# First layer's attention: ScalarE writes the fp16 high halves of two of five weight blocks by a second exponential

## The reference, cut to what matters

```python
q = (hidden_states @ Wq).reshape(b, s, NUM_HEADS, HEAD_DIM)       # 4, 512, 32, 16
kv = hidden_states @ Wkv
k, v = (kv[..., :HEAD_DIM], kv[..., HEAD_DIM:])
scores = jnp.einsum('bqhd,bkd->bhqk', q, k) * scale
bias = slopes[:, None, None] * (pos[None, None, :] - pos[None, :, None])
scores = jnp.where(causal[None, None], scores + bias[None], -jnp.inf)
attn = jax.nn.softmax(scores, axis=-1)
out = jnp.einsum('bhqk,bkd->bqhd', attn, v).reshape(b, s, h)
return out @ Wo
...
x = x + _layernorm(_L0_attn_ref(_layernorm(x, axis=-1), L0_attn_Wq, L0_attn_Wkv, L0_attn_Wo), axis=-1)
x = x + _layernorm(_L0_ffn_ref(_layernorm(x, axis=-1), ...), axis=-1)
```

## Time and profile before

| | us |
|---|---|
| median of three runs | 2361.22 |
| all three | 2360.77, 2361.22, 2366.06 |
| the profiled execution | 2361.95 |
| its span, first to last instruction | 2360.2 |
| busy TensorE / VectorE / ScalarE / GpSimd | 2064.3 / 1772.9 / 1393.0 / 961.4 |

### The profile page before, as it was taken

The page is one execution under the profiler, slowest core; times in us unless marked ns, Lnnn a source line. Parts: engine busy times, 40 slices in busy tenths (PEclk is TensorE's granted clock), DMA queues, the critical chain, the costliest instruction groups (busy, mean ns, idle before and its releaser), DMA issues. The chain is left out here.

```text
span 2360.2 us, 46322 instructions
## 1 busy us (share of the span) xinstructions
PE 2064.3 (87%) x17280; PEld 1236.9 (52%) x17280; DVE 1772.9 (75%) x3704; ACT 1393.0 (59%) x3030; POOL 961.4 (41%) x966
## 2 busy tenths in 40 slices
PE   7576687878765579999999999999999999988998
PEld 3244455555542245666656665656665666543444
DVE  5577888888765367787778787877787878877665
ACT  3344455564544367777778777777777777752222
POOL 1056766776783133323332333332333333343221
PEclk9788898989887799999999999999999999999999
DMA  6101010100101333543545344434444444430000
GB/s 228 39 10 32 15 45 15 46 13 13 40 1 45 108 73 69 95 86 68 95 86 95 74 80 93 88 68 91 84 96 70 87 82 85 86 94 19 36 18 36
DMA packets 394816, 153.70 MB, mean 65 GB/s; under 512 B 363152, under 2 KB 374032, under 8 KB 392544
## 3 DMA queue, kind: packets, MB, share of 16 engines
q1 hardware_dynamic: 394592, 150.73, 29.5%
HBM read 48.69 MB, written 11.53 MB: 26 GB/s over the span
## 5 line engine op out<-in xcount | busy, mean ns | idle before, releaser
L1629 POOL TENSOR_TENSOR q_in_sbuf<-q_in_sbuf,sinq 128x512 f32<-128x512 f32 x128 | 162.6, 1271 | 724.6 <-ACT q_in_sbuf L1761 603.0
L1773 ACT ACTIVATE xp<-xp,nm 128x128 f32<-128x128 f32 (+3 forms) x512 | 281.3, 550 | 200.4 <-DVE nm L1854 200.4
L789 ACT ACTIVATE weights<-bank,unit 128x512 f32<-128x512 f32 x320 | 210.5, 687 | 269.7 <-PE bank L592 268.3
L1738 ACT ACTIVATE probs_hi<-xp,rl 128x128 f16<-128x128 f32 (+3 forms) x512 | 245.1, 550 | 64.8 <-DVE rl L1874 64.8
L1825 DVE SCALAR_TENSOR_TENSOR probs_lo<-xp,rl,probs_hi 128x128 f16<-128x128 f32 (+3 forms) x512 | 282.5, 613 | 0.0
L513 POOL CAST weights_hi<-weights 128x1024 f16<-128x1024 f32 (+1 forms) x192 | 213.0, 1122 | 157.0 <-ACT weights L789 139.6
L1833 DVE TENSOR_TENSOR q1T_lo<-qf,q1T_hi 128x512 f16<-128x512 f32 x128 | 88.4, 691 | 227.8 <-ACT q1T_hi L1752 227.8
L1854 DVE CUSTOM_DVE_ANT_0 xp<-bank,mask,cs 128x128 f32<-128x128 f32 (+3 forms) x512 | 250.4, 545 | 0.0
L1655 PE MATMUL bank<-p1T_hi,v_hi 128*128 128x128 f16 x1280 | 221.5, 219 | 2.6 <-DMA p1T_lo<-probs_lo 2.6
L1655 PE MATMUL bank<-p1T_hi,v_lo 128*128 128x128 f16 x1280 | 221.4, 219 | 0.0
L1655 PE MATMUL bank<-p1T_lo,v_hi 128*128 128x128 f16 x1280 | 221.4, 219 | 0.0
(11 more groups left out here) (317 smaller groups left out, 5795.2 us busy)
## 6 DMA issues: line engine op xcount, KB each, us to landing
raw_q<-in_wq SPq DMA_DIRECT2D x8, 1024.0 KB, 6.3
raw_o<-in_wo SPq DMA_DIRECT2D x8, 1024.0 KB, 6.4
x_front<-in_x SPq DMA_DIRECT2D x4, 1024.0 KB, 5.7
q_stack<-q_hi SPq DMA_DIRECT2D x256, 16.0 KB, 1.8
xb<-in_x SPq DMA_DIRECT2D x4, 1024.0 KB, 5.2
wup<-in_wup SPq DMA_DIRECT2D x3, 1024.0 KB, 11.2
fused_scratch<-fused SPq DMA_DIRECT2D x12, 256.0 KB, 2.9
x_scratch<-xb SPq DMA_DIRECT2D x3, 1024.0 KB, 4.3
```

Source lines behind the costliest of these rows:

```text
L789: act.activation(px[:, p % 2, i, :], bank_of(("x", p, i))[:, :], ACT.Exp, scale=unit[:, 0:1]).then_inc(s_ed, 1)
L1629: pool.tensor_tensor(qs[:, i % 2, :], qs[:, i % 2, :], rope["sink" if u[0] == "k" else "sinq"][:, :], ALU.mult).then_inc(s_rot, 1)
L1738: ins = act.activation(pr[0][:, m % 2, c], xp[:, m % 3, c], ACT.Copy, scale=rl[:, m % 3, t:t + 1])
L1773: ins = act.activation(x, x, ACT.Exp, scale=-1.0, bias=nm[:, m % 3, t:t + 1], accum_out=ls[:, m % 3, t:t + 1])
```

## The change

ScalarE writes blocks 3 and 4 of a pair twice: once as fp32 into `px`, and once more, by the same exponential of the same bank, as fp16 into `ph[0]`. GpSimd then casts only blocks 0 to 1 and 2, and subtracts for blocks 3 and 4 in one call of 1024 columns. VectorE's second subtraction is only block 2, 512 columns. The waits follow: ScalarE waits at block 3 for GpSimd's low halves of the pair two before, and for that pair's value products, since it now writes `ph[0]`; GpSimd waits for the fifth exponential instead of its own casts; a pair has two casts to count, not three.

```diff
                 def weights_hi(p):
                     if p >= 2:
                         pool.wait_ge(s_pf, p - 1)
-                    for i, (c0, c1) in enumerate(((0, 2), (2, 4), (4, 5))):
+                    for c0, c1 in ((0, 2), (2, 3)):
                         pool.wait_ge(*emptied[("x", p, c1 - 1)])
                         pool.tensor_copy(ph[0][:, p % 2, c0:c1, :], px[:, p % 2, c0:c1, :]).then_inc(s_wh, 1)
-                    pool.wait_ge(s_wh, 3 * p + 3)
-                    pool.tensor_tensor(ph[1][:, p % 2, 4, :], px[:, p % 2, 4, :], ph[0][:, p % 2, 4, :],
+                    pool.wait_ge(*emptied[("x", p, 4)])
+                    pool.tensor_tensor(ph[1][:, p % 2, 3:5, :], px[:, p % 2, 3:5, :], ph[0][:, p % 2, 3:5, :],
                                        ALU.subtract).then_inc(s_wc, 1)
...
                 def exponential(p, i):
-                    if p >= 2 and i in (0, 2, 4):
-                        act.wait_ge(*((s_wl, 2 * (p - 2) + 1), (s_wl, 2 * (p - 2) + 2), (s_wc, p - 1))[i // 2])
+                    if p >= 2 and i in (0, 2, 3):
+                        act.wait_ge(*{0: (s_wl, 2 * (p - 2) + 1), 2: (s_wl, 2 * (p - 2) + 2), 3: (s_wc, p - 1)}[i])
+                    if p >= 2 and i == 3:
+                        act.wait_ge(s_pf, p - 1)
                     act.wait_ge(*filled[("x", p, i)])
-                    act.activation(px[:, p % 2, i, :], bank_of(("x", p, i))[:, :], ACT.Exp,
-                                   scale=unit[:, 0:1]).then_inc(s_ed, 1)
+                    ins = act.activation(px[:, p % 2, i, :], bank_of(("x", p, i))[:, :], ACT.Exp, scale=unit[:, 0:1])
+                    if i >= 3:
+                        ins = act.activation(ph[0][:, p % 2, i, :], bank_of(("x", p, i))[:, :], ACT.Exp,
+                                             scale=unit[:, 0:1])
+                    ins.then_inc(s_ed, 1)
...
                 def weights_lo(p, i):
-                    c = slice(2 * i, 2 * i + 2)
-                    dve.wait_ge(s_wh, 3 * p + i + 1)
+                    c = slice(2 * i, 2 + i)
+                    dve.wait_ge(s_wh, 2 * p + i + 1)
```

## The result

The changed kernel takes 2369.39 us (median of 11 runs, 2367.82 to 2372.73) against 2362.22 us before (11 runs, 2356.94 to 2366.06). The ratio is 1.0035, with a 95% interval of 1.0026 to 1.0043: slower by 7.2 us. The profiled execution has a span of 2366.1 us, 5.9 more than before.

A forecast was written before the change was run, and what follows sets the result against it. VectorE, 83% busy, was taken as nearest to the bound, with ScalarE's copy order and SyncE's DMA queue as other chains. The terms -11.6 + 14.3 + 5 gave +7.7 us, hence 2369 us; range 2346 to 2386.

The forecast's parts named there:

- VectorE's gain, -11.6: First layer's attention after 276 us: VectorE's shorter second subtraction releases TensorE earlier in some steps, 11.6 us saved.
- the rival's 20: Rival A's gain: 0.57 us counts in 83% of the 42 steps after 276 us, 20 us in all.
- ScalarE's order, +14.3: Extra exponentials stand before ScalarE copies that VectorE and TensorE wait for, in the first layer's attention: 14.3 us lost.
- The port, +5: VectorE's subtractions and GpSimd's longer 2.2 us subtraction exclude each other: 5 us lost, bounds -10 and +25.
- rival C: The port lock dominates: VectorE's first subtraction meets GpSimd's 2.2 us block, mean above 1.6 us; 2389 us; chance 0.08.
- 36 or more: Sign expected in the profile after: VectorE's busy time down 36 us or more.
- two signs of being wrong: First: VectorE's waits for ScalarE's high halves not growing about 0.5 us each; second: SyncE's chain binding after 276 us too.
- upper bound of +25: Port term's upper bound: half a microsecond lost in each of 50 steps, 25 us.
- A: VectorE is the bound and ScalarE's slack real: 2341 us, or 2349 in a half form; chance 0.22 with that form.
- B: Losses on ScalarE and port equal the gains within 7 us: 2361, between 2354 and 2368; chance 0.30.

The follow-up runs named there:

- third run: The kernel before with only VectorE's second subtraction cut to block 2, ScalarE and GpSimd unchanged: 2347.78 us, ratio 0.9949.
- the split one: GpSimd's 1024-column subtraction made in two calls of 512: the changed kernel so edited took 2366.98 us, and without ScalarE's second exponentials 2351.99 us.
- the fills: The changed kernel without second exponentials, GpSimd's subtraction replaced by two fills of the same 1024 columns that read nothing: 2346.52 us, ratio 0.9928.
- first run: The kernel before with ScalarE's second exponentials of blocks 3 and 4 added alone, written to an unread tile: 2382.99 us, ratio 1.0097.
- fourth: The changed kernel with ScalarE's second exponentials moved behind the copies that follow the first ones, same instructions: 2360.82 us, ratio 1.0002.
- second run: The changed kernel without ScalarE's second exponentials, GpSimd's 1024-column subtraction kept: 2360.97 us, ratio 1.0001.
- eighth: The changed kernel with second exponentials behind the copies and GpSimd's subtraction in two calls of 512: 2351.23 us, ratio 0.9956.
- sixth: The changed kernel without second exponentials and with GpSimd's subtraction in two calls of 512: 2351.99 us, ratio 0.9959.

## Why the prediction was right, and which terms were not

**The total.** Forecast 2369, measured 2369.39. The directions were right, but two terms were off by 6 to 8 us each, in opposite directions. That the total fits to half a microsecond is luck.

**VectorE's gain, -11.6.** Right. Alone it is -12.8 us, though the third run's higher clock (0.9492 over all its runs, 0.946 before) has a part in that. The 512-column call takes 0.67 to 0.68 us where nothing blocks it, where I took 0.65, and the gain is far below the rival's 20, as TensorE waits for VectorE only in some steps.

**ScalarE's order, +14.3.** The mechanism is right: the waits for the high halves grew by 16.2 us, 11.9 of them by the second exponentials, the order alone takes 8.6 us of the loss away, and the waits go with it. The size depends on what stands beside it. Adding the second exponentials costs 2369.39 - 2360.97 = 8.4 us beside GpSimd's one long call, and 2366.98 - 2351.99 = 15.0 beside the split one. That the 14.3 is close to the second figure doesn't help it, since the changed kernel has the one long call.

**The port, +5.** This is the step that was mis-sized: "I count 0.3 to 0.8 us in a third of 50 steps, 5 us". Without the second exponentials it is 13.2 us, and 14.4 by the fills, the lower clock included. I looked only at the two big subtractions, and between them the waits did not grow: in the changed kernel's trace the group lost 185.2 - 144.7 = 40.5 us, more than 64 x 0.57 = 36.5. The mean of the first stayed at 1482 ns, below the 1600 that I had named as rival C's mark. Without the second exponentials, where the 13 us were measured, the 512-column form does wait, with a mean of 944 ns. And in both I missed tiny VectorE instructions that read one small tile, before and after:

```profile
L968 DVE COPY mx<-mp 128x8 f32<-128x8 f32 x15 | 8.9, 596 | 0.6 <-DVE mx L966 0.2
L890 DVE TENSOR_SCALAR ve<-mv 128x4 f32<-128x4 f32 x14 | 4.1, 292 | 0.5
```

```profile
L973 DVE COPY mx<-mp 128x8 f32<-128x8 f32 x15 | 13.9, 926 | 0.6 <-DVE mx L971 0.2
L895 DVE TENSOR_SCALAR ve<-mv 128x4 f32<-128x4 f32 x13 | 10.5, 807 | 0.4
```

Together 13.0 us became 24.4. The first of them feeds the maxima's transpose, the second the norms, so both stand at the head of a chain. Without the second exponentials they are 13.0 and 9.5 us, with fills in place of the subtraction 6.8 and 5.1. How much of the 13 us they make, beside the 16.5 us of the big subtractions and the clock, is not shown. My sum had no term for the clock at all.

**How they fit.** Why is the sum -13 + 13 + 8 and not -13 + 13 + 15? A likely reason: the second exponential delays the long call by 0.58 us, and in the last steps VectorE's 512 columns are then over before it begins. In the changed kernel these rows stand so, VectorE and then GpSimd:

```profile
696.94 0.67 DVE L965 TENSOR_TENSOR weights_lo<-weights,weights_hi 128x512 f16<-128x512 f32 x1
...
697.22 2.38 POOL L515 TENSOR_TENSOR weights_lo<-weights,weights_hi 128x1024 f16<-128x1024 f32 x1 [3.08 <-ACT weights_hi L793]
```

GpSimd is the one that waits here. VectorE's 512-column calls sum to 49.9 us in the changed kernel and to 60.4 without the second exponentials, 10.5 more, which fits. That this is the whole of the 7 us is argued, not shown. So the total came out right because a port term too small by 8 us met a ScalarE term too large by 6.

**The signs.** The second exponentials are there, 128 with a mean of 689 ns, and VectorE's 512-column call takes 0.68 us unblocked. VectorE's busy time, though, fell by 27.3 us and not 36 or more (469.96 to 442.70, from 120 us to the last copy of head sums), since the tiny instructions took 11.4 of the 40.5 us back and others some more. Of the two signs of being wrong, the first did not come: the waits for high halves grew by 0.46 us each. The second did in part. After 276 us TensorE waited 6.9 us in 4 places for the maxima's DMA before, at most 2.6, and waits 14.2 in 6 now, the longest here:

```profile
607.01 0.61 PE L590 MATMUL bank<-q_stack,k_stack 128*128 128x512 f16 x1 [5.51 <-DMA q_stack<-m_lo]
```

The third run, with VectorE's part alone, has such a wait of 5.46 us too. So SyncE's queue can bind after 276 us as well once VectorE is faster, and my gain had no term for that. The range was also narrower than the prediction says: with the port at its upper bound of +25 its own sum gives 2389, outside 2386.

**The rivals.** A is refuted by the first run: alone ScalarE's work costs 22 us. Its slack is real only behind the copies, where the same work costs nothing (fourth against second run, eighth against sixth). B, a cancellation within 7 us, missed by little; it holds for VectorE against GpSimd, which cancel within 1 us. C had the right pair of engines, but neither the instruction nor the size: the first subtraction's mean stayed at 1482 ns, and the port's price is 13 us, not 25.

## What to carry to other kernels

An engine that is 55% busy can be the wrong place for more work: what counts is which instruction of it others wait for next. Put the added work behind the copies that release other engines; here that order is worth 8.6 us with the same instructions. And work moved from VectorE to GpSimd should go in short calls, since VectorE can be shut out for the length of one: two calls of 512 columns in place of one of 1024 are worth 9 us here where nothing else hides it. When two runs are compared stretch by stretch, read the granted clock of the stretch first: here 5.5 of 7.7 us were TensorE's busy time at a lower clock.

## What the runs showed of the hardware that I had not expected

A VectorE copy of 8 columns takes 174 ns unblocked and up to 1755 ns beside GpSimd's long subtraction; a `tensor_scalar` of 4 columns takes 169 ns and up to 2133:

```profile
L973 DVE COPY mx<-mp x16: 174/935/1755, 104.3 to 669.3; 128x8 f32<-128x8 f32 x16
```

```profile
L895 DVE TENSOR_SCALAR ve<-mv x15: 169/417/2133, 104.1 to 727.3; 128x4 f32<-128x4 f32 x15
```

(minimum, median and maximum in ns.) The longest of them, VectorE and then GpSimd, end together:

```profile
666.94 2.13 DVE L895 TENSOR_SCALAR ve<-mv 128x4 f32<-128x4 f32 x1
...
666.92 2.12 POOL L515 TENSOR_TENSOR weights_lo<-weights,weights_hi 128x1024 f16<-128x1024 f32 x1
```

They have one SBUF input each, so the exclusion is not only a matter of two inputs. The Trainium skill (SBUF — State Buffer, Who interferes with whom) names copies and `tensor_scalar` among the instructions that can take the shared pair, if their operands meet certain conditions; these rows agree, even at 4 columns. Not every GpSimd instruction blocks them: the copy at 395.82 took 0.17 us while GpSimd's reciprocal square root of 128x4 ran from 395.57 to 396.61. A GpSimd subtraction of 1024 columns took 2.12 us where nothing blocked it (estimated: 2.15), and a fill of 1024 fp16 columns 952 ns in the mean.
